# Selection products for the maxima of four batches in place of two, with newly ordered instruction lists

## The reference

```python
h = layernorm(x)                                   # over the 256 channels
q, k, v = h, ctx, ctx    seen as (batch, 8 heads, 16 rows, 256)
s    = SCALE * log(k_length)                       # one factor per batch
attn = softmax(s * einsum('bhdq,bhdk->bhqk', q, k))
x    = x + einsum('bhqk,bhdk->bhdq', attn, v)
n    = layernorm(x)
probs = softmax(n @ w_router.T)                    # 2 experts
a    = square(leaky(n @ w_fc.T, 0.5))              # 1024 hidden per expert
x    = x + top_weight * (a @ w_proj.T of the expert with the larger logit)
```

## Time and profile before

| | |
|---|---|
| median of 3 runs | 177.59 us (177.4 to 178.49) |
| the profiled execution's own time | 180.15 us |
| its span, first to last instruction | 177.6 us |
| PE, DVE, ACT, POOL busy | 163.7, 135.9, 96.2, 59.0 us |
| granted TensorE clock | full in all 40 slices of the page |

### The profile page before, as it was taken

One profiled execution on the slowest core, in us unless ns is written; L12 is line 12 of the kernel. 1 busy time (PEld: TensorE's weight loads), 2 busy tenths in 40 slices (PEclk: granted clock), 3 DMA queues, 4 the chain that ended last, 5 costly groups with the idle time before them and its releaser, 6 DMA issues.

```text
span 177.6 us, 4052 instructions
## 1 busy us (share of the span) xinstructions
PE 163.7 (92%) x1478; PEld 140.3 (79%) x1478; DVE 135.9 (77%) x300; ACT 96.2 (54%) x181; POOL 59.0 (33%) x69
## 2 busy tenths in 40 slices
PE   7489998998989979989998999999999989999992
PEld 7478766677867758768697869888888889999992
DVE  6589978799999999988788787675683786553451
ACT  4275689553986564528664942284498034462230
POOL 4527625100724542001642512032524022463220
PEclk9999999999999999999999999999999999999999
DMA  4945786778550610460156116000310000010001
GB/s 118 284 146 188 223 272 212 223 237 235 150 167 26 162 52 0 153 148 0 32 172 185 30 61 181 4 0 0 94 59 0 4 0 0 0 63 0 0 0 59
DMA packets 19458, 17.49 MB, mean 98 GB/s; under 512 B 1840, under 2 KB 19248, under 8 KB 19440
## 3 DMA queue, kind: packets, MB, share of 16 engines
q1 hardware_dynamic: 18720, 16.52, 31.0%
q10 hardware_dynamic: 720, 0.73, 1.4%
HBM read 8.72 MB, written 1.05 MB: 55 GB/s over the span
## 4 chain that ended last, share of the span: by engine, by line
PE 62%; DVE 16%; DMA 6%; SPq 6%; issue 5%; ACT 3%; DVEq 0%; ACTq 0%
PE hp L1354 19%; PE ops L1384 17%; PE stp L1314 5%; PE pv L1338 5%; DVE negm L815 4%; PE snp L1261 4%; PE ops L1269 4%; DMA x_raw<-x 3%; ACT probs L516 3%; SPq L175 2%; DMA k_st<-k_hi 2%; DVE wproj_lo L950 2%; SPq L184 2%; PE ops L1372 2%; DMA q_st<-mx 2%
## 5 line engine op out<-in xcount | busy, mean ns | idle before, releaser
L379 POOL TENSOR_TENSOR a_buf<-l_buf 128x512 f32<-128x512 f32 x32 | 35.7, 1118 | 76.4 <-ACT l_buf L524 60.0
L516 ACT ACTIVATE probs<-stp,scale_b 128x1024 f32<-128x1024 f32 x30 | 33.4, 1115 | 13.5 <-PE stp L1314 10.8
L815 DVE TENSOR_REDUCE negm<-snp 128x4 f32<-128x1024 f32 x28 | 34.1, 1218 | 6.8 <-PE snp L1261 6.4
L1354 PE MATMUL hp<-xt_hi,wfc_hi 128*128 128x256 f32 x128 | 37.4, 293 | 0.5 <-issue 0.5
L1354 PE MATMUL hp<-xt_hi,wfc_lo 128*128 128x256 f32 x128 | 35.8, 279 | 0.0
L1354 PE MATMUL hp<-xt_lo,wfc_hi 128*128 128x256 f32 x128 | 35.7, 279 | 0.0
L918 DVE TENSOR_TENSOR a_lo<-a_buf,a_hi 128x512 fp32r<-128x512 f32 x32 | 26.3, 824 | 7.2 <-ACT a_hi L531 7.0
L524 ACT ACTIVATE l_buf<-hp 128x512 f32<-128x512 f32 x32 | 19.0, 592 | 20.8 <-PE hp L1354 20.2
L1354 PEld LDWEIGHTS hp<-xt_hi,wfc_hi 128*128 128x128 f32 x128 | 24.0, 188 | 2.7 <-issue 1.1
L1354 PEld LDWEIGHTS hp<-xt_hi,wfc_lo 128*128 128x128 f32 x128 | 24.1, 188 | 0.0
L1354 PEld LDWEIGHTS hp<-xt_lo,wfc_hi 128*128 128x128 f32 x128 | 24.1, 188 | 0.0
(11 more groups left out here) (111 smaller groups left out, 241.5 us busy)
## 6 DMA issues: line engine op xcount, KB each, us to landing
wfc_raw<-w_fc_t SPq DMA_DIRECT2D x8, 256.0 KB, 4.3
k_st<-k_hi SPq DMA_DIRECT2D x16, 128.0 KB, 2.6
wproj_raw<-w_proj_t SPq DMA_DIRECT2D x8, 256.0 KB, 3.7
q_st<-q_hi SPq DMA_DIRECT2D x14, 128.0 KB, 2.2
x_raw<-x SPq DMA_DIRECT2D x8, 128.0 KB, 2.8
k_st<-k_lo SPq DMA_DIRECT2D x8, 128.0 KB, 2.5
v_raw<-ctx_t SPq DMA_DIRECT2D x8, 128.0 KB, 2.8
x_keep<-x SPq DMA_DIRECT2D x8, 128.0 KB, 2.8
```

The source lines that it names most:

```text
L379: pool.tensor_tensor(a_buf[d % 2][:, :, :], l_buf[d % 2][:, :, :], l_buf[d % 2][:, :, :], ALU.mult).then_inc(s_a, 1)
L516: act.activation(probs[g][:, :, :, :], pair[:, :, :].rearrange("p e (c n) -> p e c n", c=KC), ACT.Exp, scale=scale_b[:, b:b + 1]).then_inc ...
L815: dve.tensor_reduce(negm[b % 2][:, :, :, g].rearrange("p c e -> p e c"), pair[:, :, :].rearrange("p e (c n) -> p e c n", c=KC), AX.X, ALU. ...
L1354: last = pe.matmul(hp[:, d % 2, half], wfc[w][:, kc, c * P:(c + 1) * P], xt[:, kc, :], start=(c % 2 == 0 and kc == 0 and w == 0 and xt is ...
```

## The change

`ROWS_FROM = 4` replaces the literal 2 in every test of the kind `b < 2` that chooses between selection products and stack rows. Batches 2 and 3 therefore run `scores_kq` with 8 matmuls per pair of heads in place of 4, use 128-row maxima (`nm_rows`, `max_transpose`, `max_rows`), and drop `stack_max(2)`, `stack_max(3)`, `clear_max(4)` and `clear_max(5)`; `stack_pick` moves to the batches 4 and 5. The low part of batch 0's keys is made on VectorE (`split_first_k`) and not on GpSimd. The calls of all five engines are written in a new order.

```diff
+ROWS_FROM = 4
         def stack_pick(q, j):
-            q.wait_ge(s_st, PAIRS * (j + 1))
+            q.wait_ge(s_st, PAIRS * (j + ROWS_FROM - 1))
...
-                if b < 2:
+                wait(act, s_st, PAIRS * (b - 1))
+                if b < ROWS_FROM:
                     act.activation(mx[j][:, :], ...)
...
+            def split_first_k():
+                dve.wait_ge(s_khi, 1)
+                dve.tensor_tensor(k_lo[0][:, :], kv_raw[0][:, :], k_hi[0][:, :].bitcast(f32), ALU.subtract).then_inc(s_klo, 1)
...
             def scores_kq(b, g):
-                    if b < 2:
+                    if b < ROWS_FROM:
                         pe.wait_ge(s_mrows, b + 1)
                     else:
-                        pe.wait_ge(s_mxst[j], 16 * (b // 2))
+                        pe.wait_ge(s_mxst[j], 16 * (b // 2 - 1))
...
-                    if b >= 2:
+                    if b >= ROWS_FROM:
                         continue
...
```

In the DMA queue the first two weight loads stood ahead of the first key stacks, and now the first stands behind them:

```diff
             load_x(sp, 1)
-            load_weights(sp, 0, 0)
-            load_weights(sp, 0, 1)
             stack_k(sp, 0, 0)
             stack_k(sp, 0, 1)
             stack_k(sp, 0, 2)
+            load_x(sp, 2)
             load_kv(sp, 2)
-            load_weights(sp, 0, 2)
+            load_weights(sp, 0, 0)
+            load_v(0)
+            stack_k(sp, 1, 0)
...
```

More of the change, by code:

```diff
@@ new lines, in _ @@
+            router(1)
+            split_max_hi(3)
+            split_w_lo(1, 0)
+            split_max_lo(3)
+            pv_turn(2)
+            neg_logit(0)
+            den_inverse(2)
+            x_newton(6, 1)
+            attention_out(2)
+            neg_abs(0)
+            split_w_lo(1, 1)
+            attention_turn(2)
+            x_moments(7, 2)
+            row_max(4, 0)
+            x2_sum(2)
+            row_max(4, 1)
+            square_lo(0, 1)
+            x2_moments(2, 0)
+            x2_moments(2, 1)
@@ L1314, in scores_kq @@
                         last = pe.matmul(pair[:, e, kc * DIM:(kc + 1) * DIM], k_st[j][rows, g, kc * P:(kc + 1) * P],
[L1315 to L1316 removed]
+                                         q_st[j][rows, g, :], start=(kc == 0), stop=(b >= ROWS_FROM), skip_group_check=True)
+                    if b >= ROWS_FROM:
                         continue
@@ L1525, in _ @@
             max_transpose(4)
-            ffn2(0, 8)
-            ffn1(0, 15)
-            ffn2(0, 9)
-            ffn2(0, 10)
-            ffn2(0, 11)
-            ffn2(0, 12)
-            scores_qk(5, 0)
+            ffn1(0, 11)
+            ffn1(0, 12)
+            ffn2(0, 2)
+            ffn2(0, 3)
+            ffn2(0, 4)
+            ffn1(0, 13)
+            ffn2(0, 5)
+            scores_qk(5, 0)
+            scores_kq(4, 0)
+            ffn1(0, 14)
+            ffn1(0, 15)
+            scores_kq(4, 1)
+            scores_qk(5, 1)
             x_transpose(1)
-            scores_kq(4, 0)
-            ffn2(0, 13)
-            scores_qk(5, 1)
-            scores_kq(4, 1)
+            ffn2(0, 6)
+            scores_kq(4, 2)
+            scores_qk(5, 2)
+            ffn2(0, 7)
             ffn1(1, 0)
@@ L1574, in _ @@
             max_transpose(6)
+            ffn1(1, 10)
+            ffn2(1, 1)
+            ffn2(1, 2)
+            ffn2(1, 3)
             ffn2(1, 4)
+            ffn1(1, 11)
             ffn2(1, 5)
```

859 lines of the change are left out of this document (412 added, 447 removed).

## The result

| | before | changed |
|---|---|---|
| median of the runs shown together | 178.04 us (177.4 to 178.85, 4 runs) | 172.36 us (172.29 to 172.59, 4 runs) |
| profiled execution: own time, span | 180.15, 177.6 | 172.33, 170.4 |
| first scores | 11.20 | 8.07 |
| last exponential of batch 1 | 30.74 | 29.54 |
| first `ffn1` | 41.57 | 41.94 |

The ratio is 0.9681, with a 95% interval of 0.9634 to 0.9728: faster by 3.2%. Where the runs of one kernel spread, a ratio and its interval go by its fast ones, those within 1.5% of the fastest.

The account below looks back on a forecast made before the run. It took VectorE and TensorE as both full from the first `ffn1` to the second transpose, then TensorE alone. First `ffn1` at 44.0 + 129.3 of TensorE + 3.3 to the span's end = 176.6 us, range 173.4 to 179.9.

Parts of the forecast that it names:

- the first `ffn1` at 44.0: Start of the first `ffn1`: taken as 44.0 from two estimates, 44.5 and 43.4, with ends 42.2 and 47.2.
- rival A: Ahead of `ffn1`: the lead is kept as idle VectorE time takes the new work; `ffn1` at 42.2, 174.5 us; chance 0.33.
- second reckoning: VectorE ahead of `ffn1`, by work alone: +4.35 of work less the lead of 2.5, so `ffn1` at 43.4.
- The first reckoning: Start to `ffn1`, operation by operation: last exponential of batch 1 at 31.5, `x2n1` at 42.3, `ffn1` at 44.5.
- 129.3 us behind the first `ffn1`: TensorE from the first `ffn1` on: 132.8 us before, changes of -1.7 + 1.2 - 2.3 - 0.75, so 129.3.
- the waits for VectorE, 2.0 in three, stay: TensorE's three waits for VectorE, 2.0 us together, were to remain unchanged.
- six score passes and one transpose, 7 x 0.24: TensorE behind `ffn1`: these passes of batches 2 and 3 are done earlier, -1.7 us.
- the tie: At the second transpose: VectorE's work falls to 29 us and TensorE's to about 28, so no wait added or removed.
- Blocks: Score blocks between expert pieces: each costs 0.46 us beyond its contents; 26 become 21, -2.3 us.
- The wait for batch 5's key stack: TensorE at 78.34: a wait of 0.75 us goes, since `clear_max(5)` ahead of it in the queue is gone.
- B: From `pv_turn(0)` to `x2n1`: VectorE is late, losses put `ffn1` at 47.2, 179.8 us; chance 0.20.
- C: Nothing that counts moves: 1.1 us of 3.05 saved return as VectorE waits at the second transpose, 177.7 us; chance 0.12.

Follow-up runs that it names:

- the two experiments with pairs: Changed kernel with one pair of score steps of batches 2 and 3 moved back behind the first `ffn1`: 174.79 us; with two pairs: 177.46 us.
- the two with the cut: Eight VectorE `square_lo` subtractions cut to 8 of 256 columns per half: kernel before, 176.93 us; changed kernel, 172.08 us, or 171.58 with the added memsets late.

## Why the prediction was wrong

**What it said of the start: right in kind, too mild in size.** First scores 8.4 (8.07), first exponential 16.4 (15.80). The conversion was priced at 0.3 and took 0.17 in place of 1.27, once no GpSimd memset ran beside it. The Trainium skill (SBUF — State Buffer, Who interferes with whom) describes how a cast of VectorE and a GpSimd instruction can shut each other out for a whole instruction; the pair of rows agrees, though no row shows in which mode the cast ran.

**First step that failed: the first `ffn1` at 44.0; it came at 41.94,** on the side of the prediction's own sign for rival A (before 42.5). The terms of the second reckoning, by VectorE's work, can be read off: 41.57, less a lead of 3.13 (2.5 in the forecast), plus 30.93 - 27.18 = 3.75 of work (4.35), less 0.25 of idle, is 41.94. This adds up by construction; what it shows is which terms were off, the lead and the work by 0.6 each. The first reckoning, step by step, put the last maximum of batch 1 at 23.1 (21.89) and its last exponential at 31.5 (29.54): the first exponential came 0.6 earlier, the maximum followed it by 6.1 us (6.7 in the walk), and the last exponential followed the maximum by 7.65 (8.4). Taking the middle of the two reckonings added 0.6 to the error. Rival A's 42.2 for this row was right, though its reason, idle that fills, accounts for only 0.25. How far VectorE's work sets this row is shown on one side only: 4.6 us more of it made the kernel 3.45 us longer at full clock, but a microsecond less of it, and a maximum less, brought nothing.

**Second step that failed: 129.3 us behind the first `ffn1`; it was 125.2** (like the forecast's figure, to the end of the last matmul). The sum took 2.8 us of work and 0.75 of waiting off TensorE. Measured by the rows by stretch, its busy time fell by 4.7 and its idle time by 2.9. The term "the waits for VectorE, 2.0 in three, stay" is the one that failed most clearly: the two of them that lay behind `ffn1`, 1.71 us, went, and so did 0.67 for `x2n` and 0.6 for a stacked maximum, against about 1.0 of new ones (`nm_r` 0.49, `wproj_lo` 0.54). The term "six score passes and one transpose, 7 x 0.24" counts TensorE's passes alone, which is right for the passes: by the forecast's prices a pair costs 0.48 + 0.23 for its products + 0.46 for its block = 1.17, and put back its own work took 1.10. But it cost 2.14, and two 4.07. Over three pairs the excess is 2.9 us of the 4.1 by which the step was off (the third by the same price, an estimate), and all of it is waits; some of them are so short that the view counts them as busy. What was left out is when a pair's maximum can start: VectorE does it, 1.2 us, ahead of `ffn1`, where the forecast had charged it, and the turns of maxima behind wait less. That the waits hang on this start, and not on how much VectorE has to do, is argued from the two experiments with pairs and the two with the cut; no run moved a maximum alone. The forecast saw the work go ("from some 36, to 29"; it was 25.75, with 3.1 more of it behind the second transpose), and then put "neither add nor remove one" on the tie, so that it charged the work ahead of `ffn1` and credited nothing behind it.

**Blocks.** 0.46 each was a good size for what a block costs TensorE: about 0.4, measured twice. With the waits that seven more of them brought it was 0.62. Five blocks give 2.0 to 3.1 in place of 2.3.

**The wait for batch 5's key stack** went as forecast. The products' price was right too: in the changed kernel the step from the start of a pass with products to the next pass is 0.58, and 0.34 without, so 0.24 (0.23 in the forecast).

```profile
43.52 0.39 PE L1318 MATMUL stp<-q_st,k_st 64*128 64x256 f32 x2
...
44.10 0.40 PE L1265 MATMUL snp<-k_st,q_st 64*128 64x256 f32 x4
...
55.43 0.50 PE L1265 MATMUL snp<-k_st,q_st 64*128 64x256 f32 x4
55.77 0.28 PE L1318 MATMUL stp<-q_st,k_st 64*128 64x256 f32 x2
```

Together with the waits for the stacked maxima, which I had called covered, this side gave more than the sum: in the old lists the products were expected to cost a microsecond and seem to be worth 0.7.

**The base.** The sum ended in a span and was read as a time. Runs have 1.7 to 3.0 us around the span, mostly 1.9, and the execution shown was longer than the median by as much, so the two cancelled: the sum said -1.0 and the typical span fell by 5.2 to 6.0. It also hides where the gain is. The old lists reach their first `ffn1` near 40.6 at full clock, with first scores near 10.2. Against that the new start leads by 2.1 us and not 3.1, the changed kernel is 1.3 us behind when the experts begin, and all that it wins it wins in the dense stretch, 7.2 to 7.6 us.

**Rivals.** B (VectorE late) did not come: the longest of VectorE's small operations ahead of `x2n1` took 0.52 us. C needed new waits of 1.1 at the second transpose, and there are none. One more reason for the gain is not tested by itself: VectorE's operations ran shorter beside GpSimd, 6.7 us in all. The cut, which took 4.0 and 4.5 us of VectorE's work out of the dense stretch, bounds what that can be worth there at under 2 us. What stays open: the other 1.2 of the 4.1 us, how it divides between waits for DMA and small gaps, and what a kernel with a third pair behind `ffn1` would take.

## What to carry to other kernels

When a unit of work moves ahead of a barrier, price it on every engine that it touches, and credit behind the barrier what you charge ahead of it. A tie of two engines is tested by loading and by relieving one, which no busy share shows: here 4.6 us more cost 3.2 and 4.5 less gave about 1, since relief can give back no more than the idle time that is left. Count the blocks in an edited list before dividing by them. A feature that is worth little in the old order can be what a new order needs, so try it in both. And look where a profiled execution is longer than the median before using its rows as a base.

## What the hardware showed

- A switch of TensorE between 64-row and 128-row passes and back costs about 0.4 us, with no wait in it: seven more of them made TensorE busy for 2.8 us more and took 4.3 us with what waited behind them.
- TensorE's granted clock fell to half, its 1.2 GHz level, in stretches after it had been idle: 0.53 after a window with 2.04 us of 6 busy, 0.50 after one with 2.43 of 4. One and the same kernel took 174.6 us at a mean clock of 1.000 and 181.7 at 0.952, and the eight runs between fall in with their clock. With the new start, where TensorE is busy for all of 4 to 12 us, all four runs had 0.999 to 1.000.
- A VectorE conversion of 8 columns took 1.27 us beside a GpSimd memset that ended with it, and 0.17 without.
